# One batch's cross-attention moved into the feed-forward stage of a decoder layer, with two more feed-forward units among the last attention step

## What is computed

```
x = layernorm(x + attn(x))          # 16 heads: q, k, v, gate, s projections; a recurrence over the
                                    # tokens with 64 slots a head, softmax over slots; Wo
x = layernorm(x + xattn(x, ctx))    # query, key = ctx @ Wq.T + bq, ctx @ Wk.T + bk   (128 wide)
                                    # attention = softmax(query @ key.T, axis=-1)     (512 x 512)
                                    # x_m = x @ attention
x = layernorm(x + ffn(x))           # gate, up = quant(x) @ ternary(w).T              (2048 wide)
                                    # h = silu(gate) * up; y = quant(hadamard(h)) @ ternary(w_down).T
```

## Time and profile before

| | |
|---|---|
| median of 3 runs | 1534.14 us (1532.18 to 1534.96) |
| profiled execution, its own time | 1532.19 us |
| span of the profile, first to last instruction | 1530.4 us |
| TensorE (PE) busy | 1489.3 us (97%) |
| VectorE (DVE), ScalarE (ACT), GpSimd (POOL) busy | 1043.8, 649.3, 433.3 us |
| mean granted TensorE clock | 0.996 |

### The profile page before, as it was taken

How to read it: one execution, slowest core, us unless ns; L and a number is a source line. 1 busy time by engine, 2 the same in 40 slices (tenths; PEclk the granted TensorE clock), 3 DMA queues, 4 the chain that set the end, 5 groups by cost and what they waited for, 6 DMA issues and landing times.

```text
span 1530.4 us, 24190 instructions
## 1 busy us (share of the span) xinstructions
PE 1489.3 (97%) x9538; PEld 1206.5 (79%) x9570; DVE 1043.8 (68%) x1990; ACT 649.3 (42%) x1247; POOL 433.3 (28%) x282
## 2 busy tenths in 40 slices
PE   8999999999999999999999999999999889999998
PEld 6888888888888888888888888877878645666675
DVE  5666655665556666656665677787777976877887
ACT  5333333333323333333434334334333346867775
POOL 0211011210214444434454323221321134323320
PEclk9999999999999999999999999999999999999999
DMA  4511111120202222222233202101200403544552
GB/s 153 179 60 58 42 49 56 57 68 29 76 11 80 70 70 75 71 70 69 83 104 90 84 21 70 49 8 35 63 28 29 165 35 118 159 131 134 160 167 92
DMA packets 107584, 121.17 MB, mean 79 GB/s; under 512 B 5328, under 2 KB 75088, under 8 KB 107344
## 3 DMA queue, kind: packets, MB, share of 16 engines
q1 hardware_dynamic: 104016, 113.33, 23.4%
q10 hardware_dynamic: 3456, 6.29, 1.1%
HBM read 92.34 MB, written 27.26 MB: 78 GB/s over the span
## 4 chain that ended last, share of the span: by engine, by line
PE 88%; DVE 6%; issue 2%; ACT 2%; POOL 1%; DMA 1%; POOLq 0%; SPq 0%; DVEq 0%; ACTq 0%
PE bank L448 18%; PE bank L454 17%; PE bank L451 17%; PE bank L676 6%; PE bank L574 4%; PE bank L691 3%; PE bank L711 3%; PE bank L509 2%; PE bank L536 2%; PE bank L582 2%; PE bank L560 2%; PE bank L531 1%; PE bank L517 1%; PE bank L524 1%; PE bank L568 1%
## 5 line engine op out<-in xcount | busy, mean ns | idle before, releaser
L448 PE MATMUL bank<-Wh,X 128*128 128x512 f32 x512 | 211.5, 413 | 0.8 <-DVE X1l L1196 0.7
L454 PE MATMUL bank<-Wh,X 128*128 128x512 f32 x512 | 201.7, 394 | 0.0
L451 PE MATMUL bank<-Wl,X 128*128 128x512 f32 x512 | 200.7, 392 | 0.0
L802 ACT ACTIVATE V<-bank 128x256 f32<-128x256 f32 x128 | 49.0, 383 | 322.4 <-PE bank L454 322.4
L1380 POOL TENSOR_TENSOR sm<-sm,half 128x8 f32<-128x8 f32 x32 | 52.7, 1648 | 396.3 <-DVE sm L1096 396.2
L448 PE MATMUL bank<-X,Wh 128*128 128x512 f32 x384 | 157.0, 409 | 7.5 <-ACT Wh L757 5.8
L451 PE MATMUL bank<-X,Wh 128*128 128x512 f32 x384 | 150.8, 393 | 0.0
L454 PE MATMUL bank<-X,Wl 128*128 128x512 f32 x384 | 150.7, 393 | 0.0
L1362 POOL TENSOR_TENSOR Wl<-RAW,Wh 128x512 fp32r<-128x512 f32 (+1 forms) x65 | 112.2, 1735 | 128.9 <-ACT Wh L757 128.9
L1403 POOL TENSOR_TENSOR LO<-M,HI 128x512 fp32r<-128x512 f32 x64 | 82.1, 1282 | 148.3 <-PE bank L685 117.4
L676 PE MATMUL bank<-XT,W 128*128 128x512 bf16 x495 | 117.2, 379 | 4.4 <-DVE M L1252 3.4
(11 more groups left out here) (190 smaller groups left out, 3317.3 us busy)
## 6 DMA issues: line engine op xcount, KB each, us to landing
z_scratch<-EV SPq DMA_DIRECT2D x64, 256.0 KB, 2.0
Z<-z_scratch SPq DMA_DIRECT2D x16, 1024.0 KB, 5.9
RAW<-wgT SPq DMA_DIRECT2D x16, 512.0 KB, 3.9
RAW<-wuT SPq DMA_DIRECT2D x16, 512.0 KB, 3.7
RAW<-wdT SPq DMA_DIRECT2D x16, 512.0 KB, 3.6
RAW<-Wo SPq DMA_DIRECT2D x14, 512.0 KB, 3.7
RAW<-Wv SPq DMA_DIRECT2D x26, 256.0 KB, 2.9
RAW<-Wg SPq DMA_DIRECT2D x26, 256.0 KB, 3.3
```

What stands on the lines that cost most here:

```text
L448: engine.matmul(o, lh(c), rh(c), start=c == 0, stop=False)
L451: engine.matmul(o, lh(c), rl(c), start=False, stop=False)
L454: last = engine.matmul(o, ll(c), rh(c), start=False, stop=c == n - 1)
L802: engine.activation(V[:, par, i, :], bk[:, 0:256], ACT.Copy).then_inc(S["v_evac"], 1)
```

## The change

1. For the last batch (b = 3), rounded context and query and key lie in the memory of the down weights, `W3[:, 2]`, in place of `X1h` and `ATh` (new lists `CHL` and `QK`, indexed by batch). So `ctx` of that batch waits for the last projection instead of for `xm3` of batch 2, and `qk_out` waits for GpSimd's last `Wl`. The down weights come in four transfers of 512 KB, put before the transfers of `had1_out` 14 to 17, the first behind a wait for the last `energy`.
2. `SEAM` has 17 items instead of 22 and no free places; six units are spread among the last step's stages.
3. `PLACES`: `energy`, exp and all that follows for batch 3 stand among the feed-forward units; batch 2's quantising (`x_round0` to `x_turned_out`) too, at units 6 to 10; for batch 1, `att_scale`, `att01`, `att23` stand earlier and `x_round0`, `x_made0`, `x_round1` later; smaller shifts for batches 0 and 2.
4. `UNIT`: within a unit `high` stands after `had2_out`, `had1` after `add`, `read` and `scale` earlier, `normal` a unit later. `HOLD` has new numbers.

```
-SEAM = (("states", 31), ("sums", 31), ("turn_o", 30), ("ok", 31), ("turn_ok", 31), ("y", 30), None, ("turn_w", 31),
-        None, None, ("weights", 31), None, None, None, ("values", 31), None, ("turn_o", 31), ("unit", 0), ("unit", 1),
-        ("unit", 2), ("unit", 3), ("y", 31))
-SEAM_UNITS = 4
+SEAM = (("states", 31), ("turn_o", 30), ("sums", 31), ("ok", 31), ("y", 30), ("turn_ok", 31), ("unit", 0), ("unit",
+        1), ("turn_w", 31), ("unit", 2), ("weights", 31), ("unit", 3), ("values", 31), ("unit", 4), ("turn_o", 31),
+        ("unit", 5), ("y", 31))
+SEAM_UNITS = 6
...
     dict(ctx=444, centre=444, qk=446, n1=448, qk_out=448, x101=449, x101_out=450, energy=450, energy_out=451,
-         x123=453, att_scale=453, x123_out=454, att01=455, att01_out=456, att23=456, att23_out=457, xm0=459,
-         xm0_out=460, xm1=462, xm1_out=463, xm2=463, xm2_out=464, xm3=464, xm3_out=465, x_round0=465, x_made0=466,
-         x_round1=469, x_made1=474, x_turned=475, x_turned_out=476),
+         att_scale=451, x123=453, att01=453, x123_out=454, att01_out=454, att23=454, att23_out=457, xm0=459,
+         xm0_out=460, xm1=462, xm1_out=463, xm2=463, xm2_out=464, xm3=464, xm3_out=465, x_round0=468, x_made0=470,
+         x_round1=472, x_made1=474, x_turned=475, x_turned_out=476),
...
-    dict(ctx=500, qk=503, qk_out=504, energy=506, energy_out=507, att_scale=507, att01=510, att01_out=511,
-         att23=511, att23_out=512, centre=518, n1=522, x101=525, x101_out=526, x123=527, x123_out=528, xm0=530,
-         xm0_out=532, xm1=532, xm1_out=533, xm2=534, xm2_out=535, xm3=536, xm3_out=537, x_round0=538, x_made0=539,
+    dict(ctx=499, qk=502, qk_out=504, centre=518, n1=520, energy=522, energy_out=523, x101=524, att_scale=524,
+         att01=525, x101_out=526, att01_out=526, att23=526, x123=527, att23_out=527, x123_out=528, xm0=529,
+         xm0_out=530, xm1=531, xm1_out=533, xm2=534, xm2_out=535, xm3=536, xm3_out=537, x_round0=538, x_made0=540,
...
-UNIT = (("absmax", 25), ("had1_out", 5), ("high", 2), ("gate", 0), ("clamp", 30), ("h", 1), ("store", 38), ("low", 2),
-        ("had1", 4), ("turn_q_out", 32), ("had2_out", 24), ("read", 20), ("round", 29), ("gs", 0), ("scale", 28),
-        ("add", 35), ("normal", 36), ("turn_q", 31), ("had2", 23), ("down", 33), ("silu", 0))
+UNIT = (("absmax", 25), ("had1_out", 5), ("read", 20), ("gate", 0), ("clamp", 30), ("h", 1), ("scale", 28), ("store",
+        38), ("low", 2), ("turn_q_out", 32), ("had2_out", 24), ("round", 29), ("high", 2), ("gs", 0), ("add", 35),
+        ("had1", 4), ("normal", 37), ("turn_q", 31), ("had2", 23), ("down", 33), ("silu", 0))
...
-HOLD = (("o", 12), ("en", 9), ("y", 7), ("vg", 9), ("xm", 10), ("gate", 7), ("up", 7), ("h1", 7), ("h2", 7), ("down",
+HOLD = (("o", 12), ("en", 11), ("y", 7), ("vg", 9), ("xm", 11), ("gate", 7), ("up", 8), ("h1", 7), ("h2", 8), ("down",
...
-        CH, CL = X1h[:, 0:2], X1h[:, 2:4]
-        QK = ATh[:].rearrange("p (k s) t -> p k s t", k=2)
+        W3R = W3[:, 2, :].bitcast(R)
+        CHL = [X1h[:].rearrange("p (s c) t -> p s c t", s=2)] * 3
+        CHL += [W3R[:, 0:2048].rearrange("p (s c t) -> p s c t", s=2, c=2)]
+        QK = [ATh[:].rearrange("p (k s) t -> p k s t", k=2)] * 3
+        QK += [W3R[:, 2048:4096].rearrange("p (k s t) -> p k s t", k=2, s=2)]
...
-                    act.wait_ge(S["xm"], 4 * b)
-                    engine.activation(CH, CTX[:], ACT.Copy).then_inc(S["ctx_hi"], 1)
+                    if b < 3:
+                        act.wait_ge(S["xm"], 4 * b)
+                    else:
+                        act.wait_ge(S["proj_vg"], 4 * STEPS)
+                    engine.activation(CHL[b][:, 0], CTX[:], ACT.Copy).then_inc(S["ctx_hi"], 1)
...
+                        if b < 3:
+                            act.wait_ge(S["xm"], 4 * b)
+                        else:
+                            act.wait_ge(S["w_lo_g"], 6 * (LOADS - 1))
...
-            sp.wait_ge(S["w_lo_g"], 6 * (LOADS - 1))
-            engine.dma_start(W3[:, 2, :], scratch[2]).then_inc(S["w3_in2"], 16)
             for stage, n in (*seam_order(), *ffn_order()):
                 if stage == "had1_out":
                     b, j = divmod(n, 16)
+                    if 14 <= n < 18:
+                        sp.wait_ge(S["energy"], 4 * NB)
+                        o = slice(2048 * (n - 14), 2048 * (n - 13))
+                        engine.dma_start(W3[:, 2, o], scratch[2][:, o]).then_inc(S["w3_in2"], 16)
```

More of the change, by code:

```diff
@@ L135 @@
 PLACES = (
-    dict(ctx=397, centre=400, n1=406, qk=407, qk_out=409, x101=414, x101_out=415, energy=417, energy_out=418,
-         att_scale=418, x123=419, x123_out=420, att01=421, att01_out=423, att23=424, att23_out=426, xm0=430,
+    dict(ctx=396, centre=402, n1=406, qk=407, qk_out=409, x101=414, x101_out=415, energy=417, energy_out=418,
+         x123=419, att_scale=419, x123_out=420, att01=422, att01_out=424, att23=425, att23_out=426, xm0=430,
          xm0_out=431, xm1=432, xm1_out=433, xm2=434, xm2_out=435, xm3=437, xm3_out=438, x_round0=439, x_made0=441,
@@ L140 @@
     dict(ctx=444, centre=444, qk=446, n1=448, qk_out=448, x101=449, x101_out=450, energy=450, energy_out=451,
-         x123=453, att_scale=453, x123_out=454, att01=455, att01_out=456, att23=456, att23_out=457, xm0=459,
-         xm0_out=460, xm1=462, xm1_out=463, xm2=463, xm2_out=464, xm3=464, xm3_out=465, x_round0=465, x_made0=466,
-         x_round1=469, x_made1=474, x_turned=475, x_turned_out=476),
-    dict(ctx=474, centre=474, n1=476, qk=477, qk_out=478, x101=480, x101_out=481, energy=481, energy_out=482,
-         att_scale=483, x123=486, att01=486, x123_out=487, att01_out=488, att23=488, att23_out=489, xm0=491,
-         xm0_out=492, xm1=493, xm1_out=494, xm2=495, xm2_out=497, xm3=498, xm3_out=499, x_round0=500, x_made0=501,
-         x_round1=501, x_made1=503, x_turned=504, x_turned_out=505),
-    dict(ctx=500, qk=503, qk_out=504, energy=506, energy_out=507, att_scale=507, att01=510, att01_out=511,
-         att23=511, att23_out=512, centre=518, n1=522, x101=525, x101_out=526, x123=527, x123_out=528, xm0=530,
-         xm0_out=532, xm1=532, xm1_out=533, xm2=534, xm2_out=535, xm3=536, xm3_out=537, x_round0=538, x_made0=539,
+         att_scale=451, x123=453, att01=453, x123_out=454, att01_out=454, att23=454, att23_out=457, xm0=459,
+         xm0_out=460, xm1=462, xm1_out=463, xm2=463, xm2_out=464, xm3=464, xm3_out=465, x_round0=468, x_made0=470,
+         x_round1=472, x_made1=474, x_turned=475, x_turned_out=476),
+    dict(ctx=474, centre=474, n1=476, qk=477, qk_out=478, x101=479, x101_out=481, energy=481, energy_out=482,
+         att_scale=483, att01=486, x123=487, x123_out=488, att01_out=488, att23=488, att23_out=489, xm0=491,
+         xm0_out=492, xm1=493, xm1_out=494, xm2=495, xm2_out=496, xm3=497, xm3_out=498, x_round0=513, x_made0=514,
+         x_round1=514, x_made1=515, x_turned=516, x_turned_out=517),
+    dict(ctx=499, qk=502, qk_out=504, centre=518, n1=520, energy=522, energy_out=523, x101=524, att_scale=524,
+         att01=525, x101_out=526, att01_out=526, att23=526, x123=527, att23_out=527, x123_out=528, xm0=529,
+         xm0_out=530, xm1=531, xm1_out=533, xm2=534, xm2_out=535, xm3=536, xm3_out=537, x_round0=538, x_made0=540,
          x_round1=540, x_made1=541, x_turned=543, x_turned_out=544),
@@ L602, in energy @@
                 pe.wait_ge(S["qk_lo"], 2 * b + 2)
-                engine.matmul(bk[:], QK[:, 0, 0, n], QK[:, 1, 0, :], start=True, stop=False)
-                engine.matmul(bk[:], QK[:, 0, 0, n], QK[:, 1, 1, :], start=False, stop=False)
-                engine.matmul(bk[:], QK[:, 0, 1, n], QK[:, 1, 0, :], start=False, stop=True).then_inc(S["energy"], 1)
+                qk = QK[b]
+                engine.matmul(bk[:], qk[:, 0, 0, n], qk[:, 1, 0, :], start=True, stop=False)
+                engine.matmul(bk[:], qk[:, 0, 0, n], qk[:, 1, 1, :], start=False, stop=False)
+                engine.matmul(bk[:], qk[:, 0, 1, n], qk[:, 1, 0, :], start=False, stop=True).then_inc(S["energy"], 1)
             def turn_att(b, c):
@@ L1175, in cross @@
                         dve.wait_ge(S["qk_hi"], 2 * b + k + 1)
-                        dve.wait_ge(S["xm"], 4 * b)
+                        if b < 3:
+                            dve.wait_ge(S["xm"], 4 * b)
                         dve.wait_ge(S["vec_in"], 48)
-                        engine.scalar_tensor_tensor(QK[:, k, 1, :], bank("qk", b, k)[:], XB[:, k:k + 1], QK[:, k, 0, :],
+                        engine.scalar_tensor_tensor(QK[b][:, k, 1, :], bank("qk", b, k)[:], XB[:, k:k + 1], QK[b][:, k, 0, :],
                                                     ALU.add, ALU.subtract).then_inc(S["qk_lo"], 1)
```

17 lines of the change are left out of this document (9 added, 8 removed).

## The result

The changed kernel takes **1525.95 us** (median of 6 runs, 1525.28 to 1526.6), the one before 1533.22 in the same comparison (6 runs, 1532.18 to 1534.96). The ratio is 0.9948, with a 95% interval of 0.9938 to 0.9958. The forecast was 1525.5.

The account below looks back on a forecast made before the run. TensorE, 97% busy, bounds the kernel, so only its waits and half clock can change. -2 - 5 - 4.6 + 3.1 = -8.5 us on 1532.19 gives 1523.7; with 1.95 to the median, 1525.5 rounded, range 1518 to 1531.5.

Parts of the forecast that it names:

- Steps 28 and 29 (-2 and -5): Batch 1's attention rows and quantising: TensorE's waits for `XI` and `OKN` and a half clock go, -2 and -5 us.
- The give-back: Step 29: VectorE's moved 1.9 us delays `U`, so about 1 us of the 6.1 won is lost again.
- The seam (-4.6): Last step's stages with units spread among them: holes and clock of 6.8 us in place of 11.4, -4.6 us.
- The hole before `turn_o`: Seam: chain of 6.1 us from `values`, covered by 2.2 us of unit work, leaves 3.9 us, plus 2.0 half clock.
- The small terms: Seam: waits of 0.4 us for `weights` before the first bank of `qk`, and 0.5 for two after `OG`.
- The units (+3.1): Units 6 to 22 behind the seam, paced by VectorE: TensorE waits 6.5 us in place of 3.4, +3.1 us.
- the rival's point of decision of 3.6 us: Units: the half-clock rival (chance 0.08) decides from a hole of 3.6 us on; the largest before was 1.92.
- the seam's gain is eaten: Rival: energies' banks and late `M` cost 6 to 8 us, about 4 remain from steps 28 and 29; 1530, chance 0.20.
- the rival with the half clock: Rival: exp stretch and neighbouring blocks in the units halve the clock, 18 us lost for 3.4; about 1539, chance 0.08.
- The exp among the silus: Units, ScalarE: two added table loads of 1.28 us and four exps stop silu for 5.4 us; no drain counted.
- Costs at nothing: Down weights in four pieces, `high` moved within a unit, and new bank numbers where not read late: no cost.
- The sum: Whole kernel: -8.5 us on the profiled 1532.19 gives 1523.7; 1.95 more for the median gives 1525.6, rounded to 1525.5.

Follow-up runs that it names:

- experiment 4: Changed kernel with batch 3's context, query and key back in `X1h` and `ATh`, with the old waits for `xm`: 1526.04 us, ratio 0.9950.
- experiment 5: Changed kernel with silu in place of exp for batch 3's energies, softmax left out: 1524.93 us, ratio 0.9937.
- experiment 1: Changed kernel with all of batch 1's places set back to those of before: 1534.95 us, ratio 1.0008.
- experiment 6: Changed kernel with the order within a unit (`UNIT`) set back to that of before: 1527.33 us, ratio 0.9951.
- experiment 11: Changed kernel with batch 2's statistics (`centre`) and `n1` each two places later: 1533.29 us, ratio 0.9994.

## Why the prediction was right, and where it was not

**Steps 28 and 29 (-2 and -5): right.** From one turn of `OG` to the next, in the traces of before and after, step 28 gives 2.6 us and step 29 4.8; with batch 1's places alone 2.3 and 5.1. `OKN`'s hole and its half clock went together. The half clock was worth 2.7 instead of 2.5 us: from the turn of `OKN` to the 13th matmul behind it are 5.9 us before (1112.25 to 1118.15) and 3.2 now. The give-back, put at about 1, was 2.0: TensorE waits 1.89 us for `U` in place of 0.27, and 0.41 for the clamp. A wait of 0.32 us for `OKM` went besides, which the sum did not have. Of the 7.3 us that the two steps give (152.0 to 144.7 with the memory set back, where the clock stayed up), 1.0 is missing in the profile of the change, because the clock halved in step 27.

**The seam (-4.6): its working held by and large.** Predicted was 6.8 us of holes and clock in place of 11.4. The rows show 1.10, 0.24 (ahead of unit 3, by the time line) and 3.95 us of waiting and 1.8 us of clock (0.94 and 0.97 in two stretches of 20), 7.1 together. The hole before `turn_o` was forecast at 3.9, from a chain of 6.1 that took 6.14 (1212.29 to 1218.43). The small terms were off: 1.10 at `weights` in place of 0.4, and no wait behind `OG` in place of 0.5. For `CL` the prediction named two reasons, the new memory and the new order; experiment 4 shows that the order is enough.

**The units (+3.1): a cost was left out.** The waits came to 6.6 us against a forecast of 6.5, at the places named. But the prediction's sentence that the half clock followed "the holes of 3.59 and 3.98 us, not the one of 3.22", and the rival's point of decision of 3.6 us, failed: the clock fell behind the hole of 1.98 us before the energies, the stretch from 1240 to 1260 us stands at 0.91, and it cost 1.6 us (experiment 5). By holes and clock the units therefore gave back 4.8 us (6.6 less 3.4, and 1.6) against the seam's 4.3 (11.4 less 7.1). With a wait of 0.65 us for `X1l` that before has in step 30, this count gives a gain of about 0.1; the two traces show 0.9, and the other 0.8 I can't place. Forecast were 1.5. So of the rival "the seam's gain is eaten" the first half came true, at 4.8 us and not its 6 to 8, and the second did not: the steps gave their full 7, not 4. In the rival with the half clock, 5.8 us on 1534.14 make 1540, not 1539.

**The exp among the silus.** No drain is seen: what lies between load and exp is 0.01 us, between load and silu 0.02. The Trainium skill (ScalarE: Activation LUTs, What ACT_TABLE_LOAD costs) puts 1.38 us of drain on each switch. This trace does not show it at either load, ahead of it or behind it, and taking both switches out gained 1.0 us, less than the two loads.

**Costs at nothing.** The four pieces of the down weights left no wait of TensorE. The order within a unit and the bank numbers are perhaps not free of effect: experiment 1 shows a bank wait of 1.5 us that may hang on the numbers, experiment 6 stays open.

**The sum.** -8.5 was predicted on the profiled execution, -6.9 was measured on it (1532.19 to 1525.28), and -7.3 by the medians. The missing 1.6 us are, by pieces and but for rounding: 1.0 for the half clock in step 27, 0.6 for seam and units, and 0.2 for the two ends, less 0.3 that the steps gave above their 7. That the forecast of the median, 1525.5, lies only 0.45 us from the measured 1525.95 is partly luck: the working was 1.6 us too low, and the 1.95 us that were added from execution to median were 1.3 too many (0.67 in the changed kernel: 1525.95 less 1525.28).

## What to carry to other kernels

Undo each part of a large change and also make each part alone. Here the undo had its own fault (a bank wait), and only the part alone showed that seven numbers carry the gain and that the part in the title brings nothing that could be measured. When a hole is to be filled with independent work, look at the order of the engine that serves both: the cover must not wait behind the chain that it covers. And when a block of VectorE work is moved, look first at what stands behind it and at what GpSimd does at its new place: in experiment 11 the block became later by 7.1 us and longer by 4.
